# A graph layer with a residual and a layer norm: the bias added to x in place for half of the tiles

## What is computed

```python
# x: (8, 1024, 128) fp32; adj: (8, 1024, 1024) int32, values 0 and 1
# weight: (4, 128, 128); bias: (128,)
masks = (adj[None] == rel_ids[:, None, None, None])   # relations 1 to 4
h = einsum('rbnm,bmd->rbnd', masks, x)
y = einsum('rbnd,rdo->bno', h, weight) + bias
s = x + y
out = (s - mean(s)) / sqrt(var(s) + 1e-5)             # over the last axis
```

## Time and profile before

| | us |
|---|---|
| median of 3 runs | 117.33 (115.39, 117.33, 117.61) |
| the profiled execution | 115.86 |
| its span, first to last instruction | 113.8 |

### The profile page before, as it was taken

The page is one execution under the profiler, slowest core; times in us unless marked ns, Lnnn a source line. Parts: engine busy times, 40 slices in busy tenths (PEclk is TensorE's granted clock), DMA queues, the critical chain, the costliest instruction groups (busy, mean ns, idle before and its releaser), DMA issues.

```text
span 113.8 us, 1983 instructions
## 1 busy us (share of the span) xinstructions
PE 104.4 (92%) x596; PEld 86.1 (76%) x597; DVE 83.4 (73%) x220; ACT 84.6 (74%) x116; POOL 75.9 (67%) x97
## 2 busy tenths in 40 slices
PE   5958799989999999999999999999999999999910
PEld 2336696848777898989888989888989888889810
DVE  0095648438599969996999699959897989284960
ACT  0424895582996979797979797979798989894460
POOL 5032030001999899989998999799989998723570
PEclk9999999999999999999999999999999999999995
DMA  3999999999999999999999999999999999640243
GB/s 72 397 433 434 403 432 426 425 430 415 420 415 449 417 412 412 429 426 423 403 426 423 435 407 428 415 426 423 435 420 409 415 412 422 272 190 6 112 168 105
DMA packets 7363, 42.18 MB, mean 371 GB/s; under 512 B 819, under 2 KB 1206, under 8 KB 3254
## 3 DMA queue, kind: packets, MB, share of 16 engines
q1 hardware_dynamic: 7200, 41.95, 89.1%
q10 hardware_dynamic: 150, 0.07, 0.2%
HBM read 37.82 MB, written 4.19 MB: 369 GB/s over the span
## 4 chain that ended last, share of the span: by engine, by line
PE 60%; DMA 25%; DVE 7%; POOL 3%; issue 2%; POOLq 1%; DVEq 0%
PE h_ps L183 39%; DMA adj_sb<-in_adj_dram 25%; PE tp_ps L174 10%; PE y_ps L196 9%; PE y_ps L190 2%; DVE mask L446 2%; DVE stats L203 2%; POOL scale L215 2%; DVE total L453 1%; POOLq L338 1%; DVE out_sb L219 1%; DVE mean_var L208 1%; POOL var_eps L212 0%; DVE out_sb L501 0%; POOL minus_mean L310 0%
## 5 line engine op out<-in xcount | busy, mean ns | idle before, releaser
L353 ACT ACTIVATE maskT<-tp_ps 128x2048 fp32r<-128x2048 fp8e5 x32 | 60.2, 1880 | 18.8 <-PE tp_ps L174 18.8
L446 DVE TENSOR_SCALAR mask<-adj_sb 128x2048 uint8<-128x2048 uint32 x32 | 38.7, 1221 | 17.9 <-DMA adj_sb<-in_adj_dram 17.7
L183 PE MATMUL h_ps<-maskT,x_hi 128*128 128x512 f32 (+1 forms) x144 | 34.1, 379 | 0.7 <-ACT maskT L353 0.7
L183 PE MATMUL h_ps<-maskT,x_lo 128*128 128x512 f32 (+1 forms) x144 | 34.4, 381 | 0.0
L183 PEld LDWEIGHTS h_ps<-maskT,x_hi 128*128 128x128 f32 x144 | 24.2, 189 | 5.7 <-ACT maskT L353 2.0
L183 PEld LDWEIGHTS h_ps<-maskT,x_lo 128*128 128x128 f32 x144 | 24.3, 190 | 3.7
L174 PEld LDWEIGHTS tp_ps<-identity,mask 128*128 128x128 f32 x128 | 19.7, 203 | 5.5 <-DVE mask L446 2.1
L215 POOL TENSOR_TENSOR scale<-var_eps,power 128x4 f32<-128x4 f32 (+1 forms) x17 | 23.0, 1355 | 0.1
L174 PE MATMUL tp_ps<-identity,mask 128*128 128x128 f32 x128 | 20.9, 285 | 2.1 <-DVE mask L446 2.0
L212 POOL TENSOR_SCALAR var_eps<-mean_var 128x4 f32<-128x4 f32 (+1 forms) x16 | 8.4, 527 | 18.1 <-DVE mean_var L208 16.2
L196 PEld LDWEIGHTS y_ps<-w_sb,h_sb 128*128 128x128 f32 x128 | 16.6, 191 | 1.5 <-ACT h_sb L367 0.2
(11 more groups left out here) (39 smaller groups left out, 37.9 us busy)
## 6 DMA issues: line engine op xcount, KB each, us to landing
adj_sb<-in_adj_dram SPq DMA_DIRECT2D x32, 1024.0 KB, 19.8
x_sb<-in_x_dram SPq DMA_DIRECT2D x8, 512.0 KB, 15.6
out_dram<-out_sb SPq DMA_DIRECT2D x7, 512.0 KB, 20.0
out_dram<-out_sb SPq DMA_DIRECT2D x1, 256.0 KB, 2.8
out_dram<-out_sb SPq DMA_DIRECT2D x2, 128.0 KB, 1.9
w_sb<-in_L_gnn_weight_dram ACTq DMA_DIRECT2D x1, 64.0 KB, 7.3
bias_rows<-in_L_gnn_bias_dram ACTq DMA_DIRECT2D x3, 0.5 KB
```

The source lines that it names most:

```text
L183: last = nc.tensor.matmul(h_ps[:, bank, 0:n], (x_hi, x_lo)[part][:, slot, t, :], maskT[:, places, t // WORD, t % WORD, :], start=(first an ...
L353: nc.scalar.activation(maskT[:, u % NMT], turned_codes(u % NTP), ACT.Copy, accum_out=counts[:, u:u + 1]).then_inc(expanded, 1)
L446: nc.vector.tensor_scalar(mask[:, u % NMASK], adj_sb[:, u % NADJ].bitcast(u32), CAP, SET, ALU.min, ALU.mult).then_inc(masked, 1)
```

## The change

VectorE adds the bias to x in place for tiles 2 and 3 of each half (tiles 2, 3, 6 and 7 of a batch), one instruction per batch over 128 x 1024 values (two pieces of 2 tiles), in iteration `hf = 2*b`, between measuring and normalizing; for batch 0 before the loop. It waits until x_lo of that batch is made from the untouched x. The bias as fp32 rows comes from a product of TensorE into `y_ps` at the start, which VectorE copies into `bias_pair` (2 tiles). `spread_bias` in each half then covers tiles 0 and 1 only, 256 columns. In the last half, the quarter that takes x by TensorE has the bias already in x and its own bias product is dropped.

```diff
+        bias_pair = sb("bias_pair", [P, O, D], fp32)
...
             def add(b, y, tiles, count, by):
                 dve.wait_ge(projected, count)
+                dve.wait_ge(biased, b + 1)
...
+            def copy_bias():
+                dve.wait_ge(bias_spread, 1)
+                nc.vector.tensor_copy(bias_pair[:, :, :], y_ps[:, 1, 0:O, :]).then_inc(bias_copied, 1)
+
+            def add_bias(b):
+                dve.wait_ge(lo_made, 2 * (b + 1))
+                pairs = x_sb[:, b % NX].rearrange("p (h q) d -> p h (q d)", h=2)[:, :, O * D:HT * D]
+                nc.vector.tensor_tensor(pairs, pairs, bias_pair[:, :, :].rearrange("p q d -> p (q d)").unsqueeze(1).to_broadcast(
+                    [P, 2, O * D]), ALU.add).then_inc(biased, 1)
...
             convert(4)
+            copy_bias()
+            dve.wait_ge(bias_copied, 1)
+            add_bias(0)
             for hf in range(1, HALVES - 1):
...
                 measure_half(hf - 1)
+                if hf % 2 == 0:
+                    add_bias(hf // 2)
                 if hf >= 2:
                     finish_half(hf - 2)
...
             def project_half(hf):
                 if hf >= NY:
                     pe.wait_ge(added, 2 * (hf - NY + 1))
+                elif hf == 1:
+                    pe.wait_ge(bias_copied, 1)
...
-                spread_bias(y_ps[:, hf % NY], HALF[0], False).then_inc(projected, 2)
+                spread_bias(y_ps[:, hf % NY], QUARTER[0], False).then_inc(projected, 2)
 
             def place_x(b, y, tiles):
-                pe.wait_ge(x_loaded[b % NX], 16 * (b // NX + 1))
-                nc.tensor.matmul(y[:, 0:O, :], identity[:, :], x_sb[:, b % NX, tiles, :], start=False, stop=False,
+                pe.wait_ge(biased, b + 1)
+                nc.tensor.matmul(y[:, 0:O, :], identity[:, :], x_sb[:, b % NX, tiles, :], start=True, stop=False,
...
-                spread_bias(y_ps[:, (1 + c) % NY], QUARTER[0], True)
-                if c == 1:
-                    place_x(LAST, y_ps[:, (1 + c) % NY], QUARTER[2 + c])
+                if c == 0:
+                    spread_bias(y_ps[:, 1], QUARTER[0], True)
+                else:
+                    place_x(LAST, y_ps[:, 0], QUARTER[3])
...
             pe.wait_ge(bias_split, 4)
+            spread_bias(y_ps[:, 1], QUARTER[0], True).then_inc(bias_spread, 1)
             project_half(0)
```

More of the change, by code:

```diff
@@ L97, in relational_layer @@
         bias_split = sem("bias_split")
+        bias_spread = sem("bias_spread")
+        bias_copied = sem("bias_copied")
+        biased = sem("biased")
         const_set = sem("const_set")
```

## The result

| kernel | median us (runs) | ratio to before, 95% interval |
|---|---|---|
| changed, first measurement | 118.45 (4) | 1.0276 [1.0204, 1.0349] |
| changed, second | 116.95 (12) | 1.0093 [1.0059, 1.0126] |
| changed, third | 118.47 (12) | 1.0099 [1.0026, 1.0172] |

The change makes the kernel slower: by 0.9 to 1.0% in the two larger measurements, 2.8% in the first and smallest. Times of one kernel, the kernel before too, lie on two levels some 2 us apart, which in every profiled execution go with the last store landing early or late, and the ratios leave out the upper level where they can: the first measurement's four executions all lie on it, and one (118.26) is still in the third ratio.

The account below looks back on a forecast made before the run. TensorE bounded the kernel, VectorE 1.3 us a batch behind; VectorE would become the bound. Late start plus five batches of 12.05 us, less 0.2 for halved products, gave +3.2, profiled 119.1; plus 0.7 made 119.8 us, range 116.4 to 122.5.

Parts of the forecast that it names:

- rival B: Even iterations: GpSimd's L215 gets in early between the converts; 6.55 us each, 11.63 a batch, about 117.7 us; chance 0.20.
- the cost of the seven bias adds: VectorE, even iterations between measuring and normalizing: each add priced like the x_lo subtraction, 1.23 us, 1.15 of pace.
- same hand count: Even iteration from its first convert: add starts at 4.35, x_lo holds normalizations to 6.58, iteration lasts 7.07 us.
- The late start: First added bias add near 33.7 us delays the convert from 34.38 to 35.53; TensorE starts its stretch 1.15 us late.
- likeliest case: VectorE bounds the stretch at 12.05 us a batch; forecast 119.8 us, spanning 118.6 to 121; chance 0.46.
- Rival A: GpSimd does not hold the bias add up; 11.37 us a batch, about 116.9 us; chance 0.18.
- D: TensorE stays the bound and the late start is absorbed; -1.3 us, about 115.3 us; chance 0.04.
- C: Waiting x_lo subtraction splits the converts and GpSimd's scales come late; 12.6 us a batch, about 122.5 us; chance 0.12.
- signs of being wrong: Even iteration 6.3 us or less, TensorE busy throughout, or bias add far from 1.23 us; growing odd iterations: wrong size.
- line of 6.7 us: Even iterations staying under 6.7 us would decide for no holding up by GpSimd.
- Half a bias product: TensorE, each half: covering two tiles instead of four saves 0.11 us, 0.22 a batch, at most 1.3 in all.
- Copy and first add hidden at the start: VectorE, after unit 4's convert: 1.6 us, hidden by the 2.53 us adjacency wait before the convert at 24.55; cost nothing.

Follow-up runs that it names:

- the cost alone: Changed kernel with TensorE's bias product covering all four tiles again, bias adds on VectorE kept; ratio to the kernel before 1.0245.
- the gain alone: Changed kernel without any bias add on VectorE, the halved bias products on TensorE kept; ratio to the kernel before 0.9926.

## Why the prediction was right, and where not

**The bound and the mechanism: right.** VectorE became the bound by its order in the even iterations, GpSimd's cast delayed the bias add, the x_lo row got in behind it and held the normalizations, odd iterations stayed at 5.1. So it went in three of the five even iterations of the first profile (three and four in the other two); in the rest the bias add itself waited for x_lo, which is the order of rival B. The place (the bias add behind or between the converts), the holder (x_lo cut) and the pace (the cost alone) were each changed alone and answered as the mechanism demands.

**The size of the bias add: wrong, and with it the time.** The step that failed is the cost of the seven bias adds: the prediction took x_lo's 1.23 us, "1024 fp32 values". The slice takes the last 256 of 512 columns in each half of a batch, 512 values, and the text ahead of the prediction has the same error. The nearest price stood in the rows: 0.68 for the 512-column add at 42.90, or 0.60 of pace. With it the same hand count gives 4.35 + 0.60 = 4.95 where the bias add lets go, + 1.08 = 6.03 where x_lo does, + 0.49 = 6.52; measured 6.52 to 6.53 in the three iterations that went this way. In all the work ends 0.5 to 1.2 us later, not the forecast 3.2.

**The late start: wrong too.** The prediction carried 1.15 us of it to the end. It was 0.63 us (35.01 instead of 34.38) in the first profile and 0.27 and 0.29 in the other two, and in all three the wait for adjacency data, which the prediction had let go, takes it up on VectorE at 41.66 to 41.68. What is lost is lost behind that, in the even iteration from 40.10 us.

The kernel with the doubled add shows that the size was the main error: 7.06 us an iteration against 7.07, the convert of unit 29 at 95.72 against 95.78, work 3.5 us later. That the sum fits so closely there is in part luck: its late start is 0.81 and its first batch short, and the iterations of 6.55 that the sum mixes in do not come.

**The time and the chances.** 118.45 us lies in the range and near 119.8 by luck: 1.8 of its 2.4 us of span over the kernel before are the last store, for which the prediction had no term but the 0.7 us between profiled execution and median. Measured more often, the change costs about 1%, in the band to which the prediction gave 0.38 and not in that of its likeliest case. The batch of 11.61 us happens to be that of rival B (11.63), but most of it goes another way: B's order came in two of the five even iterations, with a shorter add. Rival A (no holding up) is refuted by the cut x_lo row and the rows of 1.57 us. Of D half came true, the late start does not reach the end; but TensorE did not stay the bound, as its batch of 11.33 us with the gain alone, against 11.6 here, shows. C, the worse order, did not come. Two of the prediction's own signs of being wrong did: the bias add is far below 1.23 us, and one even iteration lasts 6.25, under 6.3. Its line of 6.7 us for rival A would have misled, as 6.52 lies below it with the holding up in full.

**The smaller steps.** Half a bias product at 0.11: right. Copy and first add hidden at the start: right, 0.42 and 0.69 us, but by another wait than the one named: the convert at 20.82 waits 0.19 us for its data instead of 1.27, and that at 24.48 still 2.44 (2.53 before). The last bias add hidden behind VectorE's waits: right, 0.66 us at 102.10, and 0.95 of waiting is left before the add at 104.50. TensorE's idle time of 0.7 us a batch: 0.27, for the same mis-sized term.

## What to carry to other kernels

Count the elements of a slice before pricing it, by its shape and not by its description; here that was the difference between 1% and 3%. An instruction added to an engine that is 1.3 us from being the bound costs by its place: look which row of GpSimd runs at that moment and what both engines want next. And look at what follows the last compute row before believing a small difference: repeat until both kernels have shown both endings, and count how often each comes.

## What the runs showed of the hardware

**The holding up goes both ways for a two-operand add.** The rows before showed only GpSimd waiting for such an instruction. The changed kernel, VectorE and GpSimd:

```profile
44.75 1.44 DVE L531 TENSOR_TENSOR x_sb<-x_sb,bias_pair 128x512 f32<-128x512 f32 x1
...
44.35 1.29 POOL L170 TENSOR_TENSOR x_lo<-x_sb,x_hi 128x512 fp32r<-128x512 f32 x1
```

Free, the bias add takes 0.66; here it came 0.40 us after x_lo and took 0.78 longer, until x_lo was nearly done (45.64). The Trainium skill ("SBUF — State Buffer", section "Who interferes with whom") says that the instruction issued second blocks until the first is done; these rows agree, in this direction too.

**The last store has two landings.** What the DMA engines moved in the kernel before (its second profile, 112.5 to 117.5 us in 40 slices of 0.125 us, GB/s):

```profile
GB/s 131 0 0 0 0 0 0 8 8 8 8 8 16 8 0 0 0 0 0 0 0 0 0 0 0 0 0 0 66 0 0 0 0 0 0 0 66 0 0 0
```

After most of the store has gone, there is a gap of 0.75 us, and then eight packets come nearly one by one (8 GB/s for 0.125 us is 1 KB). The changed kernel's first profile shows the same train, its second and third none. What starts it was not found.
